# Four graph layers on one core: the setup becomes stages within the engines' orders, and all orders are new

## What is computed

```python
x = _layernorm(x + L0(x, adj))   # attention: 4 heads of 32; q, k, v, o projections with biases; masked softmax
x = _layernorm(x + L1(x, adj))   # graph attention: leaky_relu(s1_i + s2_j), masked softmax, times h = x W
x = _layernorm(x + L2(x, adj))   # the same with 8 heads of 16, plus softplus(beta_tilde) * log(adj + 1e-6); W_out
x = _layernorm(x + L3(x, adj))   # mlp1 (256), unmasked graph attention, elu, mlp2, masked graph attention, elu
```

## Time and profile before

| | us |
|---|---|
| median of 3 runs | 1126.12 |
| lowest and highest run | 1124.22, 1127.83 |
| the profiled execution's own time | 1126.89 |
| its span in the profile | 1125.1 |
| TensorE (PE) busy | 997.7, 89% |
| VectorE (DVE) busy | 917.5, 82% |
| ScalarE (ACT) busy | 734.3, 65% |
| GpSimd (POOL) busy | 397.1, 35% |

### The profile page before, as it was taken

One profiled execution on the slowest core, in us unless ns is written; L12 is line 12 of the kernel. 1 busy time (PEld: TensorE's weight loads), 2 busy tenths in 40 slices (PEclk: granted clock), 3 DMA queues, 4 the chain that ended last, 5 costly groups with the idle time before them and its releaser, 6 DMA issues.

```text
span 1125.1 us, 26002 instructions
## 1 busy us (share of the span) xinstructions
PE 997.7 (89%) x8821; PEld 727.6 (65%) x8821; DVE 917.5 (82%) x2530; ACT 734.3 (65%) x1901; POOL 397.1 (35%) x781
## 2 busy tenths in 40 slices
PE   2899888999999999999999999999999998778673
PEld 1566655858677776767676776767676867455452
DVE  4467979988899898989889998989898988876432
ACT  1698756766768686877768685867777674432522
POOL 0113233323443342625243433426252334341421
PEclk9999989999999999999999999999999999988976
DMA  4001111102020202011020202020020202010000
GB/s 121 1 11 59 39 58 29 68 20 68 29 67 11 82 15 77 20 46 52 20 72 25 67 12 76 20 72 26 31 66 11 71 17 67 20 66 20 10 0 19
DMA packets 30994, 46.77 MB, mean 42 GB/s; under 512 B 7824, under 2 KB 10128, under 8 KB 30736
## 3 DMA queue, kind: packets, MB, share of 16 engines
q1 hardware_dynamic: 30864, 45.11, 12.8%
HBM read 40.64 MB, written 4.46 MB: 40 GB/s over the span
## 4 chain that ended last, share of the span: by engine, by line
PE 34%; DVE 25%; issue 8%; POOL 4%; ACT 3%; DVEq 0%; ACTq 0%; POOLq 0%
DVE P L1147 15%; PE bank L633 8%; PE bank L592 7%; PE bank L491 4%; PE bank L538 2%; POOL e L1308 2%; DVE stats_l L1006 2%; PE bank L470 2%; PE bank L499 2%; DVE l_P L1058 1%; ACT x L769 1%; PE bank L462 1%; DVE v L1178 1%; POOL rstd_l L1274 1%; DVE h_t L1183 1%
## 5 line engine op out<-in xcount | busy, mean ns | idle before, releaser
L1147 DVE SCALAR_TENSOR_TENSOR P<-row,t2e,mask_t 128x512 f32<-128x512 f32 x512 | 358.6, 760 | 18.3 <-DMA row<-line 15.3
L724 ACT ACTIVATE probs<-probs,neg_max 128x512 f32<-128x512 f32 x256 | 183.6, 718 | 13.1 <-DVE neg_max L970 13.0
L962 DVE CUSTOM_DVE_ANT_0 probs<-bank,mask_add 128x512 f32<-128x512 f32 x256 | 168.9, 676 | 13.0 <-PE bank L491 12.9
L734 ACT ACTIVATE probs_t<-bank 128x512 f32<-128x512 f32 x256 | 149.2, 601 | 10.8 <-PE bank L499 10.8
L499 PE MATMUL bank<-ident,probs 128*128 128x128 f32 x1024 | 137.4, 275 | 13.9 <-ACT probs L724 12.6
L769 ACT ACTIVATE x<-x,shift_l,rstd_l 128x128 f32<-128x128 f32 x256 | 105.3, 483 | 62.9 <-POOL shift_l L1281 62.8
L1308 POOL TENSOR_SCALAR e<-v 128x128 f32<-128x128 f32 x128 | 77.4, 632 | 171.2 <-ACT v L816 171.2
L499 PEld LDWEIGHTS bank<-ident,probs 128*128 128x128 f32 x1024 | 114.1, 141 | 28.9 <-ACT probs L724 24.5
L1266 POOL TENSOR_TENSOR rstd_l<-mv_l,ln_eps 128x4 f32<-128x4 f32 x64 | 19.3, 302 | 298.2 <-DVE mv_l L1016 298.1
L592 PE MATMUL bank<-P,GH 128*32 128x512 f32 x1024 | 117.4, 599 | 5.5 <-DVE P L1147 2.8
L633 PE MATMUL bank<-t,l_P 128*128 128x257 f32 x512 | 119.1, 383 | 1.1 <-DVE l_P L1072 1.1
(11 more groups left out here) (161 smaller groups left out, 1901.8 us busy)
## 6 DMA issues: line engine op xcount, KB each, us to landing
row<-line SPq DMA_DIRECT2D x128, 256.0 KB, 3.7
x_in<-in_x SPq DMA_DIRECT2D x16, 256.0 KB, 2.8
out<-x SPq DMA_DIRECT2D x16, 256.0 KB, 2.0
l_P<-in_adj SPq DMA_DIRECT2D x1, 1024.0 KB, 4.8
line<-turned SPq DMA_DIRECT2D x64, 4.0 KB, 1.5
w_fc<-in_L_gnn_W_fc SPq DMA_DIRECT2D x1, 256.0 KB, 3.4
probs_t<-in_L_gnn_a_fc SPq DMA_DIRECT2D x1, 256.0 KB, 6.1
w_cat<-in_L_gnn_W SPq DMA_DIRECT2D x2, 64.0 KB, 3.4
```

The source lines that it names most:

```text
L724: act.activation(e, e, ACT.Exp, bias=neg_max[:, m:m + 1], scale=SCALE0, accum_out=g.of(den0)[:, m:m + 1])\
L734: act.activation(probs_t[c % 2][:, h, :, :].rearrange("p j n -> p (j n)"), ps("l0_t", g, m)[:, :], ACT.Copy)\
L962: dve.tensor_tensor_reduce(probs[c % 2][:, h, :], ps("l0_s", g, m)[:, :], mask_add[:, c, :], 1.0, -3.0e38, ALU.add, ALU.max, row_max[:, m: ...
L1147: last = dve.scalar_tensor_tensor(P2[:, h % GROUP2, j, :], row(g, h)[:, :], g.of(t2e)[:, j, h:h + 1], mask_t[:, j, :], ALU.max, ALU.mult)
```

## The change

The setup is cut into stages that stand in `ORDER` like those of a graph. Ahead of the first graph stand only the nine loads of layer 0's projections (with `w_out`) and biases, the five transposes of the projections and their copies. The rest is:

- SyncE: `adj_load`, `late_loads` (15 loads), then the inputs.
- TensorE: `mask_T`, four turns. ScalarE: `mask_t`, four turns, and `prior`.
- VectorE: `add_mask`, `one_mask`, `fold1`, `fold2`, `fold3`, `prior_in`, `prior_out`. Each fold ends with a memset of one column that signals it.

The stages that read a mask or a folded weight wait for it in graph 0. The folded vectors are now loaded into `P2` instead of `probs_t`. The five order strings and the banks are new for all sixteen graphs.

```diff
 ORDER = {
     "pe":
-        "a0c0b0d0a1e0e0c1b1d1f0f0f0f0e0f0g0f0f0f0e0f0f0g0f0f0e1f0f0g0f0f0e1f1g0h0f1f1i0f1e1f1f1f1g1f1e1j0a2f1"
+        "a0b0c0d00000e0e000a1b1c100d1f0f0f0f0e0f0g0f0f0f0e0f0f0g0f0f0e1f0f0g0f0f0e1g0h0f1f1i0f1f1e1f1f1f1g1f1"
...
-            pe.wait_ge(s_w, 16 * N_WEIGHT_DMAS)
+            pe.wait_ge(s_proj, 16 * N_PROJECTION_DMAS)
...
-            pe.wait_ge(s_pre_dve, 2)
-            for j in range(C):
-                pe.wait_ge(s_pre_act, j + 1)
+            pe.wait_ge(s_proj_t, 1)
+
+            def mask_T(g, j):
+                pe.wait_ge(*sig("one_mask", g, 1))
+                ps = empty("mask_T", g, j)
                 for c in range(C):
-                    last = pe.transpose(bank[0][:, c * P:(c + 1) * P], adj_m[:, c, j * P:(j + 1) * P], ident[:, :])
-                last.then_inc(s_pre_pe, 1)
-            pe.wait_ge(s_setup, 2)
+                    last = pe.transpose(ps[:, c * P:(c + 1) * P], adj_m[:, c, j * P:(j + 1) * P], ident[:, :])
+                last.then_inc(filled("mask_T", g, j), 1)
...
+            def prior(g, k):
+                act.wait_ge(*sig("prior_in", g, 1))
+                act.activation(pre[:, 3:4], pre[:, 2:3], ACT.Exp).then_inc(signal["prior_exp"], 1)
+                act.wait_ge(*sig("prior_exp", g, 1))
+                act.activation(pre[:, 4:5], pre[:, 3:4], ACT.Ln, bias=1.0)
+                act.activation(pre[:, 5:6], ones[:, 0:1], ACT.Ln, bias=pre[:, 6:7]).then_inc(signal["prior_ln"], 1)
...
+            def fold3(g, k):
+                dve.wait_ge(*sig("l3_in", g, 9 * 16))
+                for q in range(2):
+                    fold_in(w3_fc[:, q, 0:1], w3_fc[:, q, 2:2 + HID], foldv[:, 512:768])
+                    fold_in(w3_fc[:, q, 1:2], w3_fc[:, q, 2:2 + HID], foldv[:, 768:1024])
+                fold_in(w3_hand[:, 0:1], w3_hand[:, 2:2 + D], foldv[:, 1024:1152])
+                fold_in(w3_hand[:, 1:2], w3_hand[:, 2:2 + D], foldv[:, 1152:1280])
+                dve.memset(folds[:, 2:3], 0.0).then_inc(signal["fold3"], 1)
...
             def l0_max(g, m):
                 c, h = m // HEADS0, m % HEADS0
                 dve.wait_ge(*wrote("l0_s", g, m))
+                if g.i == 0 and m == 0:
+                    dve.wait_ge(*sig("add_mask", g, 1))
```

More of the change, by code:

```diff
@@ L530, in l0_y, with project @@
                 last.then_inc(filled("l0_y", g), 1)
[L532 removed]
+            def project(stage, src, before, cat, width, folded):
                 def f(g, k):
@@ L621, in l3_h @@
                     pe.wait_ge(*took("l3_m1", g, 1))
+                if c == 0 and g.i == 0:
+                    pe.wait_ge(*sig("fold3", g, 1))
                 ps = empty("l3_h", g, c)
@@ L872, in _ @@
             stages = {
-                "l0_xT": xT_out("l0_xT", "l0", (("l0_q", 0), ("l0_k", 0), ("l0_v", 0))),
+                "mask_t": mask_t_out, "prior": prior, "l0_xT": xT_out("l0_xT", "l0", (("l0_q", 0), ("l0_k", 0), ("l0_v", 0))),
                 "l0_q": l0_qk("q", head_q, bias_q), "l0_k": l0_qk("k", head_k, bias_k),
@@ L1054, in f @@
                         dve.wait_ge(*sig(n + "_b", g, 3))
+                        if g.i == 0:
+                            dve.wait_ge(*took("mask_T", g, 3))
                         dve.wait_ge(*wrote(n + "_s", g))
@@ L1141, in l2_p @@
                     dve.wait_ge(*sig("exp2", g, 3))
+                    if g.i == 0:
+                        dve.wait_ge(*sig("fold3", g, 1))
                     if g.has(1):
@@ L1214, in _ @@
             stages = {
+                "add_mask": add_mask, "one_mask": one_mask, "fold1": fold1, "fold2": fold2, "fold3": fold3,
+                "prior_in": prior_in, "prior_out": prior_out,
                 "l0_v": l0_v, "l0_max": l0_max, "l0_neg": l0_neg, "l0_den": l0_den, "l0_rcp": l0_rcp, "l0_o": l0_o,
```

378 lines of the change are left out of this document (194 added, 184 removed), and 8 rows, old and new, of the table STAGES.

## The result

| | before | after |
|---|---|---|
| median of the runs, us | 1126.60 (4 runs) | 1111.39 (4 runs) |
| lowest and highest | 1124.22, 1127.83 | 1109.36, 1114.01 |
| profiled execution: own time, span | 1126.89, 1125.1 | 1113.13, 1111.3 |

The changed kernel is 15.2 us faster: ratio 0.987, 95% interval 0.984 to 0.990. That is inside the range of the forecast (1107 to 1132) but 8 us under its likeliest time, on the side of rival C.

A forecast was written before the change was run, and what follows sets the result against it. PE was taken to set the pace, with DVE next. Start -1.1, filling 0, steady state -3 and end of layer 0 -2.5 summed to -6.6, from 1126.1 to 1119.5; range 1107 to 1132.

The forecast's parts named there:

- rival C: Whole kernel: all small waits go; start -3, filling -5, steady -9, end -3, giving 1106; chance 0.13.
- The start: First graph's start: input at 20.0, first exponential at 40.7 instead of 41.25; -1.1, ends +2.6 and -3.5.
- The bank chain: Start: transposes and projections in turn through bank 6, each waiting for ScalarE's copy; 9.6 from 31.1, first exponential at 40.7.
- place 2: The use of bank 6 at the start, free at 31.1 once the first l0_max has read it.
- Loads and masks: Adjacency load and mask instructions in the setup: off the path, ready before the input; 0, or 4.9 without that cover.
- The filling: From 95 to 340, while the layers fill: nothing in the orders decides it; 0, ends -9.7 and +4.
- The steady state: Wait for ACT can shrink but need not go: 0.3 a graph off, -3 over ten graphs; ends -11 and +10.
- The end of layer 0: Graph 15's l1_o: other graphs' work covers PE's wait of 2.93; -2.5 taken, 0 as the other end.
- The tail: Graph 15's chain from l1_o on: rows in nearly the same order in both kernels; no change.
- A: Whole kernel: the start gains nothing and the new order is as good as the old; 1125; chance 0.22.
- D: Start: the input still waits behind all loads, first transpose near 24, start +2.6; 1123; chance 0.05.
- B: l2_xT to l2_h and l3_xT to l3_m1: a copy comes late, 1.0 a graph in twelve graphs; 1134.6; chance 0.20.

The follow-up runs named there:

- e3: Changed kernel with two folds and the prior moved behind graph 0's neg_max on VectorE, two exponentials moved ahead on ScalarE; 1111.19 against 1111.39.
- e6: Changed kernel with filler transposes on TensorE throughout the drain, graphs 12 to 15; 1113.00.
- e10: Changed kernel with filler transposes only where TensorE waits over 2.5 us in the drain, no more than the wait holds; 1106.18.
- e12: Changed kernel with l2_turn of graphs 4 to 13 moved later on VectorE, closer to l2_p; 1156.14.
- e2: Order alone: the old setup code ahead of everything, with the new order of all sixteen graphs; 1118.10, ratio 0.993 against the kernel before.
- e1: Setup alone: the new setup code with the old orders, setup stages at their head; 1120.69, ratio 0.995 against the kernel before.
- e5: Kernel before with one exchange on ScalarE in graphs 6 to 15, an exponential put ahead of the elu exponentials; 1123.82, ratio 0.999.

## Why the forecast was off

**The start (-1.1): failed in two places.** The input at 20.0 was right (20.03), although the adjacency landed 7.7 after its issue and not 4.8. The bank chain had one wrong link and wrong sizes. The first `l0_max` was at 29.07 and not 30.4, since the two mask transposes took 1.04 together and not 2.2. The chain from the third mask transpose (29.92, 0.63) to the prior (37.24 and 0.28) took 7.6, where I had 9.6. Of the 2.0, 1.1 is the fourth mask transpose: it is in bank 7 and not in bank 6 (place 2 says so), so it ran beside ScalarE's copy of k and cost the chain only its own copy. Another 0.8 is that the two other transposes took 0.63 each and not 1.1 and 0.95. The projections, at 1.10 each, took slightly more than the 1.0 that I had. DVE's side, `neg_max` at 37.02, was 1.4 earlier than worked out, and both ended within 0.5 of each other. By the Trainium skill (TensorE: Matmul & The Clock Gate, the part on the HAM clock gate) I had the low level as the alternative and +1 for it; the one trace of the changed kernel speaks against it and others for it. Of the six traces whose TensorE goes through this chain (after, e3, e6, e10, e12, and e2 without the mask's share) the level falls in it in four, between 32 and 41, and stays high in after and e6. None of the eight others has a fall before 44. Even at the low level the first exponential came at 38.6 (e10) and 39.0 (e12), ahead of 41.25, so the +1 was wrong too. The second place weighs more: I took the start for worth what the first exponential of the new order gains (3.8 as measured). But that mixes the two halves. Against the same order without the staged setup (e2) the first exponential is 5.7 earlier and all that follows 7.5, of which up to 3.4 are the clock that falls in e2. The setup's own value was some -5 (e1's median) to -7 and not -1.

**Loads and masks (0): right.** The masks were ready by 16.9 (12.67 and 2.17, then 2.18), before the input.

**The filling (0, ends -9.7 and +4): inside its range by the milestones, where two things nearly cancel; missed by the idle time.** Setup -6, order +5 at graph 2, sum -0.8. I had looked at the waits of PE there and not at what the deeper order does to graph 0. Counted as I had stated the term, in idle time of PE, it was not 0: from 95 to 340 PE lacks 11.0, where it lacked 20.0, so 8.9 went, of an excess that I had put at 9.7 and had left as it was. The two counts differ because the new order uses that time for the first layers of later graphs (`l0_rd` of graph 5 comes 15.1 earlier, of graph 6 21.3), which no milestone of layer 3 shows yet. By idle time the whole 13.8 are made up so: 0.7 less up to 95, 8.9 less up to 340, 10.3 less up to 840, 1.6 more behind it, and 4.6 more in which PE is busy.

**The steady state (-3, ends -11 and +10): the step that failed.** I took off 0.3 a graph; PE's idle time fell by 10.3 from 340 to 840, and a graph became 1.6 shorter. I kept the 0.83 wait of L499, since the distance behind the scores is the same in both orders (10.3 and 10.0). It went: PE's waits from 340 to 840 fell from 15.1 to 4.2 and the graph from 62.0 to 60.4, over the eight graphs to graph 10 -12.8. (The -6.5 more by graph 11 is no gain of this kind: PE has 8.6 less work in that stretch, and 6.3 come back by the end.) The distance was the wrong thing to measure. What makes that wait is ScalarE's order (the elu exponential ahead of it), as e5 shows, and I read PE's waits and not DVE's. DVE at 91% looked like a limit, but its 45.2 of idle time from 340 to 840 were waits too, the largest these:

```profile
DVE l_rden L1173 <- PE bank L633: 10.8, 10, 2.0
DVE o_t L990 <- PE bank L520: 9.5, 8, 1.2
DVE P L1147 <- DMA row<-line: 8.7, 6, 2.8
DVE x L996 <- PE bank L528: 7.5, 6, 1.3
```

In the changed kernel its idle time is 29.4. The waits for the rows are gone (over graphs 3 to 14 they were 15.3), but so are the first and the fourth of these, which are for products of PE, and the second has fallen to 4.3. e5 shows that L499's wait alone is worth at most 3.6, e12 that the new order cannot do without the distance from `l2_turn` to `l2_p`. Neither shows that this distance brings the gain, and the stretches around graphs 9 and 12 speak against its being all of it. That VectorE's waits for PE count as much was not tried. So the failed step is known, the wait and the idle time taken to stay, and the cause of the 1.6 a graph stays open.

**The end of layer 0 (-2.5): right in kind.** At graph 15's `l1_o` there is no wait any more:

```profile
928.24 3.74 PE L574 MATMUL bank<-t,l_P 128*128 128x129 f32 x32
```

**The tail (no change): failed.** From `l1_o` of graph 15 it took 174.1 before and takes 183.1. New is that graph 15 stands further ahead of graphs 12 to 14 there, and that TensorE, with less work left, is at the lower level for longer (0.77 behind 957, where it was 0.83). e10 shows that 5.2 of it can be had back by way of the level. How the 9.0 divide between the two is not shown, and executions of one order differ here by some 4 (e3 against after, above).

**The rivals.** A and D fell. B fell at its place: in the steady state PE waits for neither of the two copies; its largest wait, of the input transposes for ACT's normalised x, is 4.0 in eight graphs, 0.5 a graph, under the 0.6 from which B would decide. C gave 1106 with start -3, filling -5, steady -9, end -3; measured by the milestones of the profiled executions: filling with the start -0.8, steady -12.8, then -6.5, and +6.3 back in the drain. It had the right place for the gain, and I gave it 0.13, because I asked of DVE to follow without asking what DVE waits for.

## What to carry to other kernels

Read the waits of the second-fullest engine as closely as those of the fullest: a term kept at nothing because of one engine's waits can be wrong when the other engine's waits change. A chain of engine, transfer and engine needs its whole time (here 6 to 8 us) filled with other work. Removing one of several waits in a periodic order was worth little here (6.7 of waits, 1.9 by the medians and no difference clear of noise), since the next stood behind it; price them by an experiment, not by their sum. Where a trace is of one execution, set its time beside the median before its ends are compared. When a new order drains with less work per stage, count TensorE's lower level there, and where TensorE waits anyway, a few transposes without a reader, no longer than the wait, can pay.
